# Graph layers with edge filters on one core: a third of the filters moved from the layer stage into the product stage

## The reference, cut to what matters

```python
def ssp(x): return jax.nn.softplus(x) - LN2
bf = jnp.exp(coeff * (dist[:, None] - centers[None, :]) ** 2)
bf = ssp(bf @ W1 + b1)
bf = ssp(bf @ W2 + b2)
cut = jnp.where(dist < R_MAX, 0.5 * (jnp.cos(jnp.pi * dist / R_MAX) + 1.0), 0.0)
msg = h[src] * edge_feat * bf * cut[:, None]
agg = jax.ops.segment_prod(msg, dst, num_segments=n_nodes)
out = ssp(agg @ W3 + b3)
```

## Time and profile before

| what | us |
|---|---|
| runs of the kernel before | 5039.95, 5043.86, 5045.68 (median 5043.86) |
| the profiled execution | 5042.35 |
| its span, first to last instruction | 5040.5 |
| PE busy | 3650.4 (72%) |
| DVE busy | 3536.8 (70%) |
| ACT busy | 2398.2 (48%) |
| POOL busy | 1935.4 (38%) |

### The profile page before, as it was taken

How to read it: one execution, slowest core, us unless ns; L and a number is a source line. 1 busy time by engine, 2 the same in 40 slices (tenths; PEclk the granted TensorE clock), 3 DMA queues, 4 the chain that set the end, 5 groups by cost and what they waited for, 6 DMA issues and landing times. The chain is left out here.

```text
span 5040.5 us, 67863 instructions
## 1 busy us (share of the span) xinstructions
PE 3650.4 (72%) x20548; PEld 2062.5 (41%) x20548; DVE 3536.8 (70%) x6354; ACT 2398.2 (48%) x3982; POOL 1935.4 (38%) x1883
## 2 busy tenths in 40 slices
PE   3888887799999999999999945555555555555003
PEld 3777775355555555554555412222222222222002
DVE  7999997455555555555555268888888888888666
ACT  2666665444445444544444145555555555554003
POOL 5222000300000000000000167777777777777775
PEclk9888888899999999999999956565665566555555
DMA  3333333688888888888888756666666666666552
GB/s 115 134 132 131 126 126 128 207 264 268 262 262 261 266 270 264 262 267 273 265 273 268 208 159 177 181 178 179 177 176 181 177 179 176 180 179 171 152 158 79
DMA packets 679810, 993.87 MB, mean 197 GB/s; under 512 B 71970, under 2 KB 425111, under 8 KB 679655
## 3 DMA queue, kind: packets, MB, share of 16 engines
q1 hardware_dynamic: 588951, 857.11, 53.6%
q0 software_dynamic: 59936, 119.71, 10.1%
q10 hardware_dynamic: 30768, 15.26, 1.0%
HBM read 711.99 MB, written 279.81 MB: 197 GB/s over the span
## 5 line engine op out<-in xcount | busy, mean ns | idle before, releaser
L1362 POOL DMA_INDIRECT hgat<-x_rows,edge_src x1564 | 1532.6, 980 | 489.6 <-issue 476.4
L952 PE MATMUL bank<-gran,hp 128*128 128x490 bf16 x7056 | 1532.3, 373 | 36.0 <-DVE hp L1086 36.0
L952 PEld LDWEIGHTS bank<-gran,hp 128*128 128x128 bf16 x7056 | 679.5, 96 | 806.2 <-DVE hp L1086 38.3
L1450 PE MATMUL bank<-c_all,one_row 1*128 1x512 f32 x334 | 345.3, 1135 | 768.0 <-DVE s L1509 754.3
L805 POOL DMA_INDIRECT x_sb<-h_rows,last_i x147 | 144.5, 983 | 1835.4 <-DMA h_rows<-h_out 1764.3
L594 PE MATMUL bank<-hi_hot,lo_hot 128*128 128x49 bf16 x7840 | 573.8, 219 | 93.1 <-DVE hi_hot L430 90.9
L594 PEld LDWEIGHTS bank<-hi_hot,lo_hot 128*128 128x128 bf16 x7840 | 545.6, 155 | 216.4 <-issue 70.8
L535 ACT CAST stage<-bank 128x490 bf16<-128x490 f32 x784 | 451.4, 576 | 304.1 <-PE bank L594 296.3
L1013 DVE TENSOR_SCALAR t<-bank,c_sb 128x512 f32<-128x512 f32 x224 | 168.0, 750 | 597.6 <-PE bank L927 597.6
L1499 DVE TENSOR_SCALAR factor<-rows_e,m_same,m_first 128x128 f32<-128x128 f32 x1564 | 551.2, 352 | 42.6
L427 DVE TENSOR_TENSOR lo_hot<-lo_t,rep_lo 128x8960 bf16<-128x8960 bf16 x112 | 539.4, 4816 | 4.6 <-ACT hi_t L518 4.4
(11 more groups left out here) (229 smaller groups left out, 4725.3 us busy)
## 6 DMA issues: line engine op xcount, KB each, us to landing
gran<-step_counts SPq DMA_DIRECT2D x336, 857.5 KB, 5.1
dist<-weight_by_step SPq DMA_DIRECT2D x391, 256.0 KB, 4.6
running_products<-rows_e SPq DMA_DIRECT2D x391, 256.0 KB, 3.4
step_counts<-stage SPq DMA_DIRECT2D x112, 857.5 KB, 3.7
edge_filter_times_attr<-g_out SPq DMA_DIRECT2D x224, 256.0 KB
efl<-edge_filter_times_attr SPq DMA_DIRECT2D x224, 256.0 KB, 3.1
ef<-in_edge_attr SPq DMA_DIRECT2D x224, 224.0 KB
ef<-in_edge_attr SPq DMA_DIRECT2D x167, 256.0 KB, 3.2
```

The source lines that it names most:

```text
L952: last = nc.tensor.matmul(y, hp[:, 7 * g + i, part, :], gran[:, g, :, i * IS:(i + 1) * IS], start=first, stop=last_)
L1362: pool.indirect_dma_start(out=hgat[:, r, c, :], out_offset=None, in_=x1_d, in_offset=bass.IndirectOffsetOnAxis(ap=edge_src[:, b, c:c + 1], ...
L1450: nc.tensor.matmul(ps2[f.third()][:], one[:], c2_all[0:1, :], start=True, stop=False)
```

## The change

- `MADE_IN_C` becomes blocks below 11 and then every third (b % 3 == 1): 137 filters in the layer stage, FB = 4 slots per block, so slots exist in blocks 0 to 34 and 13 blocks have none. On PE those 13 blocks are written without the slot code, most of them in a loop (`filters=False`).
- The product stage makes ND = 254 filters, two for every three blocks from block 11 to the very last one. Its buffers for filters get four places (Q = 4) instead of three, in PSUM too: all eight banks are in use.
- `larger1` on DVE is gone. Softplus is written as the sum of Relu(z - 18), made by ACT into `excess` (bias `c1_over`), and the guarded Ln term in `a1`. PE multiplies both by `v2_sb`: eight 128 x 128 products instead of four.
- The bias goes in as one bf16 matmul with 96 rows, in which `c2` stands as three bf16 pieces; DVE makes these at the stage's start (five linked operations and three copies of one row).
- The mask copies of ACT are gone, DVE reads `edge_same` and `edge_first` in place. All loops of the product stage are written out.
- POOL has a wait more at every third block: block b = 3q waits until z2 of filter 2q - 8 is done. The edge features of a filter are loaded by two DMAs instead of one.

The core of the diff:

```diff
-MADE_IN_C = [b for b in range(NB) if b % 2 == 0 or b < ODD0 or b > C_ALL]
+MADE_IN_C = [b for b in range(NB) if b < ODD0 or b % 3 == 1]
...
-            FB = 5
+            FB = 4
...
+                        if b % 3 == 0 and 0 <= 2 * (b // 3) - 8 < ND:
+                            pool.wait_ge(s_z24, 2 * (b // 3) - 7)
...
                     def soft1(f):
-                            act.wait_ge(s_s14, f.value(1, 1))
+                            if f >= Q:
+                                act.wait_ge(s_z24, f - Q + 1)
+                            nc.scalar.activation(excess[:, f % Q], ps1[f % Q][:], ACT.Relu, bias=c1_over[:]
+                                                 ).then_inc(s_x14, 1)
...
                     def z2(f):
-                            pe.wait_ge(s_s14, f.value(1, R + 1))
-                            pe.wait_ge(s_g4, f.value(1, 1))
-                            nc.tensor.matmul(ps2[f.third()][:], one[:], c2_all[0:1, :], start=True, stop=False)
-                            for c in range(C4):
-                                last = nc.tensor.matmul(ps2[f.third()][:, c * D:(c + 1) * D], s1[:, c * P:(c + 1) * P],
-                                                        v2_sb[:], start=False, stop=c == C4 - 1)
+                            pe.wait_ge(s_l14, f + 1)
+                            pe.wait_ge(s_x14, f + 1)
+                            if f >= Q:
+                                pe.wait_ge(s_g4, f - Q + 1)
+                            z = ps2[f % Q]
+                            nc.tensor.matmul(z[:], one_b[:], c2_b[:], start=True, stop=False)
+                            for part in (excess, a1):
+                                for c in range(C4):
+                                    last = nc.tensor.matmul(z[:, c * D:(c + 1) * D], part[:, f % Q, c * P:(c + 1) * P],
+                                                            v2_sb[:], start=False, stop=part is a1 and c == C4 - 1)
...
+                    for s in range(NB):
+                        q, j = divmod(s, 3)
+                        products(s + 1)
+                        run_on(s)
+                        if j == 0:
+                            finish(2 * q - 6)
+                            finish(2 * q - 5)
```

More of the change, by code:

```diff
@@ L1219, in gnn @@
+            s_di = [sem(f"s_dist4_in{r}") for r in range(Q)]
+            s_ei = [sem(f"s_ef4_in{r}") for r in range(Q)]
             s_fi = [sem(f"s_efl_in{r}") for r in range(U)]
@@ L1305, in gnn @@
+            filter_of_block = {block_of(f): f for f in range(ND)}
+            stored_in = lambda r: 16 * len(range(r, NB, U))
+            loads_of = lambda b: 16 * sum(1 for c in MADE_IN_C if c <= b and c % U == b % U)
             with nc.Block() as block:
@@ L1435, in _ @@
-                    all_blocks(act, body)
+                    for f in range(Q):
+                        basis_of(f)
+                    for s in range(NB):
+                        q, j = divmod(s, 3)
+                        if j < 2:
+                            soft1(2 * q + j)
+                            basis_of(2 * q + Q + j)
+                        else:
+                            soft2(2 * q - 4)
+                            soft2(2 * q - 3)
                 @block.tensor
@@ L1473, in _ @@
                 def _(dve):
-                    def products(b, stage):
-                        if b.exists():
-                            r = b.ring()
-                            if b.c % 2 and stage == "both" and (b.reg is not None or ODD0 <= b.c < C_ALL):
-                                dve.wait_ge(s_fin, filter_at(b, ODD0).value(1, 2))
-                            elif b.c % 2 and (b.reg is not None or b.c > C_ALL):
-                                dve.wait_ge(s_fi[r], b.nth(16, 16 * (len(range(r, ODD0, U)) + 1 - FIRST_ALL)))
-                            else:
-                                dve.wait_ge(s_fi[r], b.nth())
-                            dve.wait_ge(s_gt[r], b.nth(16 * C4, 16 * C4))
-                            dve.wait_ge(s_sc, b.value(1, R + 1))
-                            nc.vector.tensor_tensor(prod_e[:, b.third()], hgat[:, r], efl[:, r], ALU.mult
+                    links = [0]
@@ new lines, in _ @@
+                    link(nc.vector.tensor_copy(c2_lo[:], c2_rest[:]))
+                    for p, part in ((0, c2_hi), (32, c2_mid), (64, c2_lo)):
+                        last = nc.vector.tensor_copy(c2_b[p:p + 1, :], part[p:p + 1, :])
+                    last.then_inc(s_one, 1)
+                    products(0)
+                    for s in range(NB):
+                        q, j = divmod(s, 3)
+                        products(s + 1)
[3 more added lines that the diff above has]
+                            finish(2 * q - 5)
```

382 lines of the change are left out of this document (162 added, 220 removed).

## The result

| | us |
|---|---|
| kernel before, same conditions | 5043.53 (5039.95 to 5045.68, 4 runs) |
| changed kernel | 4911.82 (4911.12 to 4912.80, 4 runs) |
| ratio | 0.974 (95% 0.9723 to 0.9757) |
| profiled execution of the changed kernel | span 4910.1 |

What follows compares the result with a forecast made beforehand. PE was taken to bound the layer stage, POOL's gathers the product stage. 5042.35 - 152.2 - 6.0 + 3.5 + 0.5 = 4888 us (ratio 0.969); own range 4866 to 4911, widened for rivals to 4860 to 4925.

Steps and rivals of the forecast that it cites:

- the slower rivals: Cases above the forecast: longer gathers (0.09), PE bounding the product stage (0.03), the change not giving back its gain (0.04).
- Gathers meet DVE more often: Product stage: gathers coincide with DVE operations more often and grow, up to +121 us; 4910 to 5009 us, chance 0.09.
- the prediction's own signs of being wrong: Product stage: POOL waiting for DVE's products or z2, gt waiting for ACT, or a gather's mean outside 964 to 995 ns.
- What bounds the kernel: PE, full at 296.8 of 300 us, bounds the layer stage; POOL's gathers, 5.15 us per block, bound the product stage.
- Part 1: Layer stage: 87 filters leave, each giving back 1.75 us of PE, -152.2 us; one wait in block 0 goes, -6.0.
- part 3: The rest: written-out loops 0, bias pieces and first loads at the product stage's start +0.5 us, last stage unchanged.
- The +1.8 us at the starts of layers 1 and 2: Layer stage: PE might wait for the last part of h, up to 2 x 0.9 us; kept only for the range.
- Part 2, the loads: Product stage, per three blocks: DVE 13.5, ACT 13.0, PE 13.2 to 14.3 us, all below POOL's 15.44.
- the rival in which it becomes the bound: Product stage: PE sets the pace and the kernel gets slower, 5091 us at 17 us per three blocks; chance 0.03.
- Part 2, the waits: Product stage: z2 and softplus finish with 13 us of room; POOL's new wait for z2 is passed at once.
- Part 2, the pace: Product stage: gathers stay at 982 ns; 48 blocks formerly without filters pay 0.07 us more each, +3.5 us.
- The bounds (-59 and +121): Product stage, gather time: -59 us if every gather takes 0.944 us, +121 if one per block meets DVE at +0.46.

Runs made afterwards that it cites:

- e3_one_psum_more: Changed kernel plus one DVE operation per filter with one PSUM and one SBUF input, output unread: 5227.44 us, ratio 0.9557 to the kernel before.
- the first four experiments: Changed kernel with gt in PSUM (5226.61 us), an added two-SBUF product (5222.38), an added one-PSUM operation (5227.44), or gt and factor in PSUM (5230.25).

## Why the prediction was right, and where it was off

The time is in the range for two reasons. The layer stage, the start and the end came as reckoned. And the range had been widened at its upper end for the slower rivals: what came in the product stage is not the forecast but the near end of *Gathers meet DVE more often*, which had a chance of 0.09. By the forecast's own range, to 4911, the time is just outside. One of the prediction's own signs of being wrong came too: the mean of a gather, 997 ns, left 964 to 995.

- *What bounds the kernel: right.* PE in the layer stage, POOL by length plus gap of its gathers in the product stage, before and after.
- *Part 1: right.* 152.2 + 6.0 was said, 157.7 with the +0.5 of part 3; 157.0 came. A slot is 1.75 us of PE and nothing took its place. The blocks with slots take 39.13 us by PE's matmuls that close a block (39.1 said), those without 32.14 (32.13), and the wait ahead of granule 4 went. The +1.8 us at the starts of layers 1 and 2 didn't come: PE's waits for `hp` in this stage went from five (36.0 us) to four (29.4 us), which is the one of block 0.
- *Part 2, the loads: right in direction.* DVE is busy 1284 of 1640 us, 78%, where 13.5 of 15.44 us were said, 87%; ACT 1242, 76%, against 84%; PE 837, 51%, within 45 to 85%. The bf16 bias took 0.557 us at the clock of this stage (0.5 said). The errors are to the cautious side, partly since operations of one engine overlap a little in the records, and cost nothing. The granted clock was 0.72 in this stretch, a mean of the two levels, and 0.58 in the same stretch before (the earlier trace rows has 0.59), with PE less busy than before (51% against 915 of 1640, 56%). So PE had more room, and the rival in which it becomes the bound didn't come.
- *Part 2, the waits: right.* On chip A POOL's own wait cost 0 (the kernel wasn't run without it, but POOL's idle time rose by 0.5 us), nothing waits for ACT, and room is left everywhere. On B, C and D "passed at once" doesn't hold, as said above.
- *Part 2, the pace: this step failed.* It said: 982 ns stay, "the nearest to it, since DVE's load per block is the same within 2%". Measured: 999 ns in the same part of the stage and 997 in all, +27.1 us instead of +3.5. The load per block was indeed the same or less. What matters is which operations it consists of. `larger1`, with one input in PSUM, went, and `efl`, with two in SBUF, came half as often again. The first holds no gather, the second does. The earlier trace rows already held the clue: the gather at 3701.72 started 0.1 us into `prod_e`, two SBUF inputs, and the one at 3707.22 before `factor`, one input. The prediction read the number of meetings from the busy share of DVE and not from the kind of operation. The bounds (-59 and +121) held it, but the chance for "gathers meet DVE more often" was put at 0.09 with "the mean is only 38 ns over the median" against it, which says nothing of what the added operations do. That the miss is only 24 us is in part luck: how long a meeting holds depends on the moment within the product, and the extra beside `efl` was 0.153 us per meeting here and 0.297 in `e3_one_psum_more`.
- *The rule that was weighed.* The prediction gave, from the Trainium skill, page "SBUF — State Buffer", section "Who interferes with whom", that a `tensor_scalar` may lock GpSimd out and that `tensor_tensor` doesn't hold up the writing of descriptors. Its reading of the earlier trace rows didn't test that: the gather at 3707.22 had started before the `tensor_scalar`. The counting says the opposite of what the prediction took from the rule: `factor` (`tensor_scalar`) 139 times 0.027 us, 3.7 us in all and never over 0.075 us, `prod_e`, `efl` and `rows_e` (`tensor_tensor`) 79.8 us of 85.9. The same section of the Trainium skill also states that a DVE instruction with two SBUF inputs contends with a GpSimd instruction that reads SBUF, and the prediction left this out. The counts agree with that sentence in every run: a gather's instruction names its row numbers, `edge_src`, which lie in SBUF. That it is this reading which is held is my conclusion and wasn't tried apart.
- *Start and end:* the start and the last stage came as said (the tail 105.0 us against 105.4).

What is shown and what isn't: that two SBUF inputs lengthen a gather, and one in PSUM doesn't, is shown by the first four experiments; the variants with `gt` and `factor` in PSUM repeat it on two more chips, the two with an added operation were run once. That the product stage on chip A grew by the gathers' length alone is the sum of its own rows (26.6 + 0.5). That `gt` in PSUM would give time back where the gathers set the pace follows from the two: the gathers got 12.7 us shorter in all on C and 21.0 us on D, so some 13 to 21 us is my estimate. It was not measured: no such chip was met again. Not tried either is whether chips B, C and D differ from A as chips or by the time at which they were used.

## To carry to other kernels

When an engine paces a stage by short instructions in a row, ask of every operation that a change adds beside it what it shares with them, not how much time it fills: here the gathers became 27 us longer with 87 more products of two SBUF inputs, 19 of it beside these products, although DVE became less busy. Where such a product can take one input from PSUM, the gathers beside it keep their length; what that is worth in time was not shown. A wait that costs nothing on one chip can be what holds the queue on another, so look for it in each trace. And a gain on the path of a full engine can be read from the trace to 1 us (1.75 us per slot), while the pace of a queue in a changed neighbourhood deserves the wider range.

## What the runs showed of the hardware

- A gather that started t us before the end of a VectorE operation with two SBUF inputs took t - 0.12 us more than 0.942 (between t - 0.108 and t - 0.129 in all 471 cases with t over 0.15 and a start over 0.045 us into the operation, chip A). If it started up to 0.04 us into the operation it kept 0.946 on average (151 cases), and the operation took longer instead: 0.74 us and not 0.69 for 512 columns.
- With a VectorE input in PSUM the extra was 0.005 us or less, over 164, 154, 98 and 160 meetings.
- The same kernel takes 5043 us on one chip and 5466, 5469 and 5513 us on others. Of the 421 us between the profiled executions on A and D, 357 lie in the product stage, 23 before it and 41 behind it. In that stage PE, ACT and DVE have stops of some 10 to 19 us, in two variants every 36 or 48 gathers. A change can be worth 0.974 on one chip and 0.952 to 0.955 on others, so a variant has to be compared with its control on the same chip.
- On those chips 250 to 342 us of GpSimd's idle time stood at one wait of its queue, at which it spent nothing on chip A.
